# A scan kernel over 16 groups: the state's product one turn later, the skip term as the output bank's seed, GpSimd's root late in the step, x times last factors on VectorE

## The chip, the cores and the metric

The kernel runs on one core of a Trainium2 chip. The metric is the device time of one execution in microseconds (us); lower is better. Five things work side by side: TensorE (PE; PEld is its weight load), VectorE (DVE), ScalarE (ACT), GpSimd (POOL), and the DMA queues, all issued by SyncE (SP). Each engine takes its instructions in program order, and waits on semaphores where it needs another's result.

## What is computed

A layer norm, then a Mamba-2 mixer, gated by a LoRA feed-forward branch, for 2 sequences of 1024 tokens with 512 channels (64 heads of 64, 8 groups, state 128):

```python
xn = _layernorm(x)
proj = einsum('bld,pd->blp', xn, in_proj_w)            # gate, x | B | C, dt
xBC = silu(causal_conv4(x | B | C) + conv_bias)
dt = softplus(dt + dt_bias); dA = exp(dt * -exp(A_log))
state = state * dA_t + (dt_t * x_t) outer B_t          # for every token t
y_t = state @ C_t
y = y + x * D                                          # the skip term
yn = rms_norm_over_group(y) * norm_weight * silu(gate)
out = x + (yn @ out_proj_w.T) * silu(ffn(xn))
```

## The kernel before

The recurrence is worked out in chunks of 128 tokens. A batch's 8 groups times 8 chunks, for 2 batches, are N = 128 turns; turn i is chunk `i % NCH` (NCH = 8) of group `i // NCH`. One loop over i is written out once for each engine, and only the order in it and the semaphores' counts decide what runs when. Inside turn i the engines also work on m = i - 1 (mixing, gating, state) and u = i - 2 (output projection, norm's scale).

For each turn:

- GpSimd computes `skip` (x times D), splits new weights into a high and a low part on some turns (`split_out` at `i % 8 == 1`, `split_conv_x` at 3, `split_gate` at 4 and 6, `split_conv_bc` at 5), computes `xw` (`scale_x`: x times each head's last decay factor), `cpre` (`left_of_state`: C times decay from the chunk's start), adds up the squares of y in two additions (`sum1`, `sum2`), takes the root (`rstd_col`, a power of -0.5) and decays the state (`sdec`).
- TensorE runs the output projection of u (`ps_out`, twelve products), the mixing product of m into the bank `ps_y` (decay matrix times `dtx`, plus `cpre` times the state before), the product of B and C (G, half of `ps_g`), the sum of squares (another part of `ps_g`), one or two blocks of the input projection for the convolution (`ps_conv`, "early" and "late", on `i % 4 != 0` and `i % 4 != 3`), a gate block (`ps_gate`) and the state's product (`ps_s`: `xw` with B, not where `i % 8 == 7`).
- ScalarE evicts a late convolution block of the turn before (L692, L693), writes the mean square (L813), Silu, eight step sizes times x (`dtx`, L831), Square of y (L841), evicts the early block, copies y's high part (`ynt_hi`), the gate's Silu; on `i % 8 == 0` it scales the new output weights (L861), on 1 splits their high part (L645), and so for the other weights.
- VectorE does the taps of the convolution (L914, three), the scan that makes the decay matrix (L1049), the last factors (`last`, L1056), a transpose (L922), y plus skip (L1091), the new state (L1097), y times gate (L1104), the scaled output added to `out_sum` (L1130, waits for `ps_out` and `rstd_col`), y's low part (`ynt_lo`, semaphore `lo2`, L1136), the early taps, and M: the decay matrix times G (L1069), which is what the next mixing product reads.

"Step k" is in this text the stretch that begins when TensorE starts the mixing product in turn i, with i mod 8 = k, and ends when it starts the next one.

`xw`, `skip`, `ps_y` and `ps_s` are single buffers. The product of the state is written for turn i:

```python
w.wait_ge(S["xw"], inner(i))
w.wait_ge(S["state"], inner(m) if m >= 0 else 0)
e.matmul(ps_s[:, :], b_tok[i % 2][:, :], xw[:, :], start=True, stop=True).then_inc(S["mm_u"], 1)
```

SyncE's queue brings decay rows (`fetch_decays`), the rows for `cpre` (`fetch_rows`), and takes x to token order through memory (`store_turned`, `fetch_tokens`: `x_tok`, `b_tok`).

## Time and profile before

| | |
|---|---|
| runs | 1863.41 us median of 3 (1862.56 to 1866.68) |
| profiled execution | 1867.85 us, span of its instructions 1866.0 us |
| TensorE busy | 1733.9 us (93%), mean granted clock 0.981 |
| VectorE busy | 1480.7 us (79%) |
| GpSimd busy | 1307.5 us (70%) |
| ScalarE busy | 1021.8 us (55%) |
| DMA | 163 GB/s mean |

An engine's share is of the whole span. TensorE's granted clock is 1.0 at 2.4 GHz. "idle before <-releaser" gives how long an engine stood ahead of an instruction and what ended it; "issue" means that the profile shows nothing.

### The profile page before, as it was taken

The page shows a single profiled execution, that of the slowest core. Times are in us where ns is not written, and L with a number is a line of the kernel's source. Part 1 is how long each engine was busy: PE and PEld are TensorE (multiplying, and loading weights), DVE is VectorE, ACT ScalarE, POOL GpSimd, SP SyncE. Part 2 cuts the span into 40 slices and gives each one's busy share as a digit, 9 for nine tenths or more (in the row PEclk, how much of TensorE's full clock was granted, in tenths as well). Part 3 has the DMA queues.
Part 4 walks back from the last instruction along what each step waited for, and adds up shares of the span by engine and source line. Part 5 has one row for each costly group of instructions (what it writes and reads, how often), then busy time and mean ns, then how long its engine had stood idle before and what let it go on. Part 6 is the DMA issues. An engine that isn't in the chain of part 4 may idle for free.

```text
span 1866.0 us, 31464 instructions
## 1 busy us (share of the span) xinstructions
PE 1733.9 (93%) x10792; PEld 1375.5 (74%) x10792; DVE 1480.7 (79%) x1839; ACT 1021.8 (55%) x2715; POOL 1307.5 (70%) x1255
## 2 busy tenths in 40 slices
PE   8979989999998999999888998999999899999986
PEld 5757767777777877777777787777777777777865
DVE  7858788787878878787877887878788787878886
ACT  4555555655555565555645655465555546555544
POOL 6537668686767858676797857669585766958576
PEclk9989999999999999999999999999999999999989
DMA  8445545555454555455775654546355454635445
GB/s 265 145 143 167 168 142 172 143 165 149 147 169 147 170 151 160 144 155 167 221 243 177 180 163 150 164 146 189 110 177 156 145 163 146 187 112 166 150 139 184
DMA packets 322415, 304.76 MB, mean 163 GB/s; under 512 B 88272, under 2 KB 255568, under 8 KB 322256
## 3 DMA queue, kind: packets, MB, share of 16 engines
q1 hardware_dynamic: 321216, 302.60, 54.1%
q8 instruction: 86, 1.41, 0.3%
q14 instruction: 73, 0.60, 0.1%
q10 hardware_dynamic: 1040, 0.16, 0.0%
HBM read 246.57 MB, written 56.10 MB: 162 GB/s over the span
## 4 chain that ended last, share of the span: by engine, by line
PE 75%; DVE 9%; issue 8%; ACT 4%; POOL 2%; DMA 2%; SPq 1%; ACTq 0%; DVEq 0%; POOLq 0%
PE ps_conv L1345 9%; PE ps_conv L1348 8%; PE ps_y L1507 6%; PE ps_conv L1351 6%; PE ps_s L1537 6%; PE ps_gate L1345 5%; PE ps_out L1348 5%; PE ps_out L1345 5%; PE ps_gate L1348 5%; PE ps_y L1512 5%; PE ps_out L1351 4%; PE ps_gate L1351 4%; DVE xc L914 2%; PE ps_conv L1352 2%; ACT dtx L831 2%
## 5 line engine op out<-in xcount | busy, mean ns | idle before, releaser
L914 DVE SCALAR_TENSOR_TENSOR xc<-ps_conv,convw_sb,xc 128x511 f32<-128x511 f32 (+2 forms) x576 | 430.4, 747 | 221.5 <-ACT xc L693 207.9
L1276 POOL TENSOR_TENSOR rstd_col<-mean_square,half 128x1 f32<-128x1 f32 x128 | 111.6, 872 | 435.8 <-ACT mean_square L813 435.6
L1049 DVE TENSOR_TENSOR_SCAN decay<-decay,eye 128x1024 f32<-128x1024 f32 x125 | 293.6, 2349 | 0.0
L813 ACT ACTIVATE mean_square<-ps_g,eps 128x1 f32<-128x1 f32 x128 | 33.4, 261 | 453.0 <-PE ps_g L1338 453.0
L1255 POOL TENSOR_TENSOR cpre<-cpre,xc 128x1024 f32<-128x1024 f32 x112 | 267.9, 2392 | 0.0
L831 ACT ACTIVATE dtx<-x_tok,prefix_dt 128x64 f32<-128x64 f32 x1024 | 257.4, 336 | 8.6 <-DMA b_tok<-turned_d 8.6
L1345 PE MATMUL ps_conv<-xn_hi,wconv_hi 128*128 128x512 f32 x768 | 258.5, 460 | 0.0
L1348 PE MATMUL ps_conv<-xn_hi,wconv_lo 128*128 128x512 f32 x768 | 214.4, 402 | 0.0
L1537 PE MATMUL ps_s<-xw,b_tok 128*128 128x512 f32 x224 | 125.4, 643 | 95.4 <-issue 75.7
L1507 PE MATMUL ps_y<-decay,dtx 128*64 128x128 f32 x1984 | 191.5, 280 | 5.0 <-DVE decay L1069 5.0
L1345 PEld LDWEIGHTS ps_conv<-xn_hi,wconv_hi 128*128 128x128 f32 x768 | 143.5, 197 | 56.6 <-issue 31.3
L699 ACT ACTIVATE xc<-xc 128x512 f32<-128x512 f32 x192 | 120.0, 627 | 112.7 <-DVE xc L914 112.7
L1348 PEld LDWEIGHTS ps_conv<-xn_hi,wconv_lo 128*128 128x128 f32 x768 | 151.0, 197 | 34.9
L1512 PE MATMUL ps_y<-cpre,state 128*64 128x128 f32 x1760 | 171.5, 273 | 0.0
L1351 PE MATMUL ps_conv<-xn_lo,wconv_hi 128*128 128x512 f32 x576 | 163.5, 392 | 0.0
L1345 PE MATMUL ps_out<-wout_hi,ynt_hi 128*128 128x512 f32 x512 | 156.6, 427 | 6.4 <-issue 4.7
L1507 PEld LDWEIGHTS ps_y<-decay,dtx 128*64 128x64 f32 x1984 | 117.4, 137 | 50.4 <-issue 38.1
L1069 DVE TENSOR_TENSOR decay<-decay,ps_g 128x1024 f32<-128x1024 f32 x125 | 151.4, 1211 | 1.2 <-PE ps_g L1338 1.2
L693 ACT ACTIVATE xc<-ps_conv,convb_sb,convw_sb 128x512 f32<-128x512 f32 (+1 forms) x192 | 149.6, 779 | 0.0
L1348 PE MATMUL ps_out<-wout_hi,ynt_lo 128*128 128x512 f32 x512 | 138.5, 392 | 1.7 <-DVE ynt_lo L1136 1.7
L1345 PE MATMUL ps_gate<-xn_hi,wgate_hi 128*128 128x512 f32 x504 | 138.6, 397 | 0.0
L1299 POOL TENSOR_TENSOR square<-square 128x256 f32<-128x256 f32 x128 | 128.1, 1001 | 13.8 <-ACT square L841 13.8
(233 smaller groups left out, 3911.9 us busy)
## 6 DMA issues: line engine op xcount, KB each, us to landing
decay<-decays_d SPq DMA_DIRECT2D x125, 512.0 KB, 5.1
cpre<-rows_d SPq DMA_DIRECT2D x112, 512.0 KB, 3.8
turned_d<-squares SPq DMA_DIRECT2D x512, 80.0 KB, 2.0
stage<-w_in_t SPq DMA_DIRECT2D x32, 1024.0 KB, 5.2
x_tok<-turned_d SPq DMA_DIRECT2D x128, 256.0 KB, 3.2
stage<-w_out_t SPq DMA_DIRECT2D x16, 1024.0 KB, 5.4
stage<-w_in_t SPq DMA_DIRECT2D x32, 256.0 KB, 3.2
b_tok<-turned_d SPq DMA_DIRECT2D x128, 64.0 KB, 3.8
```

Of the source, the lines that this page charges most:

```text
L693: e.activation(acc[:, first:], ps[:, first:], ACT.Identity, bias=convb_sb[:, tile, 0:1], scale=tap).then_inc(S["tap0"], 1)
L831: scaled = e.activation(dtx[i % 2][:, h * HD:(h + 1) * HD].rearrange("p (a i) -> p a i", i=SQ), head_of(x_tok[i % 2], h), ACT.Copy, scale= ...
L914: e.scalar_tensor_tensor(acc[:, d:], ps[:, 0:BLK - d], convw_sb[:, tile, TAPS - 1 - d:TAPS - d], acc[:, d:], ALU.mult, ALU.add).then_inc(S ...
L1049: e.tensor_tensor_scan(d, d, eye8[:, :, :].rearrange("p h i -> p (h i)"), 0.0, ALU.mult, ALU.add).then_inc(scanned(i)[0], 1)
L1069: e.tensor_tensor(by_head(d), by_head(d), ps_g[:, P:2 * P].unsqueeze(1).to_broadcast([P, GH, P]), ALU.mult).then_inc(S["M"], 1)
L1255: e.tensor_tensor(cpre[k % 2][:, :, :], cpre[k % 2][:, :, :], xc[i // CPB % 2][:, XT + 1, block_cols(i % NCH)].unsqueeze(1).to_broadcast([ ...
L1345: e.matmul(ps, a_hi(t), b_hi_(t), start=t == 0, stop=False)
L1348: e.matmul(ps, a_lo(t), b_hi_(t), start=False, stop=False)
L1351: e.matmul(ps, a_hi(t), b_lo_(t), start=False, stop=False)
L1507: mixed = e.matmul(y_h, dx[:, h * HD:(h + 1) * HD], mx[:, h * P:(h + 1) * P], start=True, stop=cm == 0, skip_group_check=True)
L1512: mixed = e.matmul(y_h, before[:, h * HD:(h + 1) * HD], c_left[:, h, :], start=False, stop=True, skip_group_check=True)
L1537: e.matmul(ps_s[:, :], b_tok[i % 2][:, :], xw[:, :], start=True, stop=True).then_inc(S["mm_u"], 1)
```

## The change

Four edits. The state's product is issued in the turn after, for m instead of i, directly behind the mixing product. The skip term is no longer added by VectorE: ScalarE's new `seed(i)` copies `skip` into the output bank `y_bank(i)`, and the mixing product adds to it (`start=False`); Square and the state's update wait for the products alone. GpSimd's root stands behind the second addition of squares instead of at the turn's start, and `skip` at the turn's start instead of near its end. `scale_x` moves from GpSimd to VectorE, behind y times gate.

```diff
--- before.py
+++ after.py
@@ -799,6 +799,13 @@
                     for q, n in rate_part(s):
                         rate(q, part_of(q, n))
 
+            def seed(i):
+
+                w.wait_ge(S["skip"], i + 1)
+                w.wait_ge(S["lo2"], i if i <= TAIL else i - 1)
+                w.wait_ge(S["sgate"], CPB if i < TAIL else N)
+                e.activation(y_bank(i)[:, :], skip[:, :], ACT.Copy).then_inc(S["seed"], 1)
+
             steps = prefix_dt[:, :, :].rearrange("p c i -> p (c i)")
             for i in range(N + DRAIN):
                 m, u = i - 1, i - DRAIN
@@ -832,7 +839,7 @@
                                               head_of(x_tok[i % 2], h), ACT.Copy, scale=steps[:, first + h:first + h + 1])
                     scaled.then_inc(S["dtx"], 1)
                 if 0 <= m < N:
-                    w.wait_ge(S["y"], m + 1)
+                    w.wait_ge(S["mm_in"], m + 1)
                     w.wait_ge(S["sum2"], m)
                     if m == 0:
                         w.wait_ge(S["mm_pt"], 2)
@@ -1069,6 +1077,16 @@
                 e.tensor_tensor(by_head(d), by_head(d), ps_g[:, P:2 * P].unsqueeze(1).to_broadcast([P, GH, P]),
                                 ALU.mult).then_inc(S["M"], 1)
 
+            def scale_x(i):
+
+                w.wait_ge(landed_tok[i % 2], 32 * (i // 2 + 1))
+                w.wait_ge(*lasts(i))
+                w.wait_ge(S["biased"], TOK)
+                w.wait_ge(S["mm_u"], inner(i) - 1)
+                weight = last_room(i)[:, :, :].rearrange("p (t h) a -> p t (h a)", t=XT)
+                e.tensor_tensor(xw[:, :].rearrange("p (t a i) -> p t a i", t=XT, a=QUADS), x_of(x_tok[i % 2]),
+                                weight.unsqueeze(3).to_broadcast([P, XT, QUADS, SQ]), ALU.mult).then_inc(S["xw"], 1)
+
             for i in range(N + DRAIN):
                 m, u = i - 1, i - DRAIN
                 cm = m % NCH
@@ -1085,10 +1103,6 @@
                         scan(i)
                     if i + 1 < N:
                         turn(i + 1)
-                if 0 <= m < N:
-                    w.wait_ge(S["mm_in"], m + 1)
-                    w.wait_ge(S["skip"], m + 1)
-                    e.tensor_tensor(y_bank(m)[:, :], y_bank(m)[:, :], skip[:, :], ALU.add).then_inc(S["y"], 1)
                 if 0 <= m < N and cm < NCH - 1:
                     new = state[(group(m) + cm) % 2]
                     w.wait_ge(S["mm_u"], inner(m))
@@ -1102,6 +1116,8 @@
                     w.wait_ge(S["square"], m + 1)
                     w.wait_ge(S["sgate"], m // CPB * CPB + CPB)
                     e.tensor_tensor(turns(y_bank(m)), turns(y_bank(m)), gate_of(m), ALU.mult).then_inc(S["yg"], 1)
+                if i < N and i % NCH < NCH - 1:
+                    scale_x(i)
                 if TAIL < i < N:
                     mixing_matrix(i)
                 if u >= 0:
@@ -1256,24 +1272,18 @@
                                 xc[i // CPB % 2][:, XT + 1, block_cols(i % NCH)].unsqueeze(1).to_broadcast(
                                     [P, GH, P]), ALU.mult).then_inc(S["cpre"], 1)
 
-            def scale_x(i):
...
             for i in range(N + DRAIN):
                 m, u = i - 1, i - DRAIN
                 f = finished(i)
-                if u >= 0:
-                    col = slice(u % 2, u % 2 + 1)
-                    w.wait_ge(S["var2"], u + 1)
-                    w.wait_ge(S["osum"], u - 1)
-                    e.tensor_tensor(rstd_col[:, col], mean_square[:, col], half[:, :], ALU.pow).then_inc(S["rstd2"], 1)
+                if i < N:
+                    nb, gi = i // CPB, group(i) % GROUPS
+                    w.wait_ge(S["silu"], max(conv_no(nb, t) for t in range(XT)) + 1)
+                    w.wait_ge(S["par"], 128)
+                    w.wait_ge(S["seed"], i)
+                    w.wait_ge(S["biased"], TOK)
+                    e.tensor_tensor(turns(skip), xc[nb % 2][:, 0:XT, block_cols(i % NCH)],
+                                    dskip_sb[:, gi * XT:(gi + 1) * XT].unsqueeze(2).to_broadcast([P, XT, P]),
+                                    ALU.mult).then_inc(S["skip"], 1)
                 if i < N:
                     g, at = divmod(i, NCH)
                     left = BATCH * GROUPS - 1 - g
@@ -1300,6 +1308,12 @@
                     w.wait_ge(S["sum1"], m + 1)
                     w.wait_ge(S["mm_ssq"], m)
                     e.tensor_tensor(square_sum[:, :], square[:, 0:P], square[:, P:2 * P], ALU.add).then_inc(S["sum2"], 1)
+                if u >= 0:
+                    col = slice(u % 2, u % 2 + 1)
+                    w.wait_ge(S["var2"], u + 1)
+                    w.wait_ge(S["osum"], u - 1)
+                    e.tensor_tensor(rstd_col[:, col], mean_square[:, col], half[:, :], ALU.pow).then_inc(S["rstd2"], 1)
+                if 0 <= m < N:
                     if cm < NCH - 2:
                         new, dec = state[(group(m) + cm) % 2], state[(group(m) + cm + 1) % 2]
                         w.wait_ge(S["state"], inner(m))
@@ -1313,15 +1327,6 @@
                         first = (cm + 1) * HEADS + gm * GH
                         e.tensor_tensor(by_head(dec[:, :]), by_head(new[:, :]), heads_bc(total_bc[:, first:first + GH]),
                                         ALU.mult).then_inc(S["sdec"], 1)
-                if i < N:
-                    nb, gi = i // CPB, group(i) % GROUPS
-                    w.wait_ge(S["silu"], max(conv_no(nb, t) for t in range(XT)) + 1)
-                    w.wait_ge(S["par"], 128)
-                    w.wait_ge(S["y"], i)
-                    w.wait_ge(S["biased"], TOK)
-                    e.tensor_tensor(turns(skip), xc[nb % 2][:, 0:XT, block_cols(i % NCH)],
-                                    dskip_sb[:, gi * XT:(gi + 1) * XT].unsqueeze(2).to_broadcast([P, XT, P]),
-                                    ALU.mult).then_inc(S["skip"], 1)
                 if i < N and i % NCH == 0:
                     edges(group(i))
                 if f is not None and not on_vector(f):
@@ -1492,11 +1497,8 @@
                 if 0 <= m < N:
                     mx, dx = decay_room(m), dtx[m % 2]
                     w.wait_ge(S["M"], m + 1)
-                    w.wait_ge(S["sgate"], CPB - 1)
                     w.wait_ge(S["dtx"], m + 1)
-                    w.wait_ge(S["lo2"], m if m < TAIL else m - 1)
-                    if m >= TAIL:
-                        w.wait_ge(S["sgate"], N)
+                    w.wait_ge(S["seed"], m + 1)
                     if cm > 0:
                         w.wait_ge(S["state"], inner(m - 1))
                         w.wait_ge(S["cpre"], later(m))
@@ -1504,7 +1506,7 @@
                     for two in range(0, GH, 2):
                         for h in (two, two + 1):
                             y_h = y_bank(m)[h % 2 * HD:(h % 2 + 1) * HD, h // 2 * P:(h // 2 + 1) * P]
-                            mixed = e.matmul(y_h, dx[:, h * HD:(h + 1) * HD], mx[:, h * P:(h + 1) * P], start=True,
+                            mixed = e.matmul(y_h, dx[:, h * HD:(h + 1) * HD], mx[:, h * P:(h + 1) * P], start=False,
                                              stop=cm == 0, skip_group_check=True)
                         if cm > 0:
                             for h in (two, two + 1):
@@ -1512,6 +1514,12 @@
                                 mixed = e.matmul(y_h, before[:, h * HD:(h + 1) * HD], c_left[:, h, :], start=False,
                                                  stop=True, skip_group_check=True)
                     mixed.then_inc(S["mm_in"], 1)
+                if 0 <= m < N and cm < NCH - 1:
+                    w.wait_ge(S["pt"], len(RATES))
+                    w.wait_ge(landed_tok[m % 2], 32 * (m // 2 + 1))
+                    w.wait_ge(S["xw"], inner(m))
+                    w.wait_ge(S["state"], inner(m - 1) if m > 0 else 0)
+                    e.matmul(ps_s[:, :], b_tok[m % 2][:, :], xw[:, :], start=True, stop=True).then_inc(S["mm_u"], 1)
                 if i < N:
                     w.wait_ge(S["silu"], max(conv_no(i // CPB, t) for t in (XT, XT + 1)) + 1)
                     w.wait_ge(S["var2"], u if u >= 0 else 0)
@@ -1526,16 +1534,7 @@
                     conv(conv_early(i))
                 for k in gated(i):
                     gate(k)
-                late_first = i < N and conv_early(i) is None and conv_late(i) is not None
-                if late_first:
-                    conv(conv_late(i))
-                if i < N and i % NCH < NCH - 1:
-                    w.wait_ge(S["pt"], len(RATES))
-                    w.wait_ge(landed_tok[i % 2], 32 * (i // 2 + 1))
-                    w.wait_ge(S["xw"], inner(i))
-                    w.wait_ge(S["state"], inner(m) if m >= 0 else 0)
-                    e.matmul(ps_s[:, :], b_tok[i % 2][:, :], xw[:, :], start=True, stop=True).then_inc(S["mm_u"], 1)
-                if i < N and conv_late(i) is not None and not late_first:
+                if i < N and conv_late(i) is not None:
                     conv(conv_late(i))
 
 
```

TensorE in the second group, at a turn with `i % 4 == 3`. Before, the state's product (`ps_s`) stands behind the gate block and ahead of the output projection:

```order
L1345 MATMUL ps_gate<-xn_hi,wgate_hi 128x512 [waits s_sgate]
L1345 MATMUL ps_gate<-xn_hi,wgate_hi 128x512 x3
L1348 MATMUL ps_gate<-xn_hi,wgate_lo 128x512 x4
L1351 MATMUL ps_gate<-xn_lo,wgate_hi 128x512 x3
L1352 MATMUL ps_gate<-xn_lo,wgate_hi 128x512
L1537 MATMUL ps_s<-xw,b_tok 128x512 [waits s_state,s_xw,s_landed_tok1]
L1345 MATMUL ps_out<-wout_hi,ynt_hi 128x512 [waits s_hi2,s_osum]
L1345 MATMUL ps_out<-wout_hi,ynt_hi 128x512 x3
L1348 MATMUL ps_out<-wout_hi,ynt_lo 128x512 [waits s_lo2]
```

After, between the mixing product of m (`ps_y`) and G (`ps_g<-xc`):

```order
L1509 MATMUL ps_y<-decay,dtx 64x128 x2
L1514 MATMUL ps_y<-cpre,state 64x128 x2
L1522 MATMUL ps_s<-xw,b_tok 128x512 [waits s_xw,s_landed_tok0]
L1342 MATMUL ps_g<-xc 64x128 [waits s_var2]
L1343 MATMUL ps_g<-xc 64x128
L1342 MATMUL ps_g<-ones,square_sum 64x1 [waits s_sum2]
L1343 MATMUL ps_g<-ones,square_sum 64x1
L1350 MATMUL ps_conv<-xn_hi,wconv_hi 128x512 [waits s_taps]
L1350 MATMUL ps_conv<-xn_hi,wconv_hi 128x512 x3
```

It has moved ahead of both products into `ps_g`, and no longer waits for the state's update there.

GpSimd in the turn with `i % 8 == 3` (`wconv_lo` is the split of the convolution's weights). Before, root first, then splits, `xw`, `cpre`, the additions, `state`, `skip`:

```order
L1276 TENSOR_TENSOR rstd_col<-mean_square,half 128x1 [waits s_osum,s_var2]
L1156 TENSOR_TENSOR wconv_lo<-stage,wconv_hi 128x512 [waits s_hi_cx] x4
L1266 TENSOR_TENSOR xw<-x_tok,last 128x512 [waits s_mm_u,s_last,s_landed_tok1]
L1255 TENSOR_TENSOR cpre<-cpre,xc 128x1024 [waits s_landed_rows0]
L1299 TENSOR_TENSOR square<-square 128x256 [waits s_square]
L1302 TENSOR_TENSOR square_sum<-square 128x128 [waits s_mm_ssq,s_sum1]
L1314 TENSOR_TENSOR state<-state,total_bc 128x512 [waits s_sdec,s_mm_in,s_state]
L1322 TENSOR_TENSOR skip<-xc,dskip_sb 128x512 [waits s_y]
```

After, the row of `skip` first:

```order
L1284 TENSOR_TENSOR skip<-xc,dskip_sb 128x512 [waits s_seed]
L1172 TENSOR_TENSOR wconv_lo<-stage,wconv_hi 128x512 [waits s_hi_cx] x4
L1271 TENSOR_TENSOR cpre<-cpre,xc 128x1024 [waits s_landed_rows0]
L1307 TENSOR_TENSOR square<-square 128x256 [waits s_square]
L1310 TENSOR_TENSOR square_sum<-square 128x128 [waits s_mm_ssq,s_sum1]
L1315 TENSOR_TENSOR rstd_col<-mean_square,half 128x1 [waits s_osum,s_var2]
L1328 TENSOR_TENSOR state<-state,total_bc 128x512 [waits s_sdec,s_mm_in,s_state]
L1284 TENSOR_TENSOR skip<-xc,dskip_sb 128x512 [waits s_seed,s_silu]
```

The root has moved behind the splits, `cpre` and both additions; `xw` is gone from this engine.

ScalarE at the turn with `i % 8 == 0` (`stage<-stage,normw_sb` scales the output weights). Before:

```order
L841 ACTIVATE square<-ps_y 128x512 [waits s_sum2,s_y]
L848 ACTIVATE ynt_hi<-ps_y 128x512 [waits s_mm_out,s_yg]
L757 ACTIVATE sgate<-ps_gate 128x512 [waits s_mm_gate]
L861 ACTIVATE stage<-stage,normw_sb 128x512 [waits s_landed_stage0]
L861 ACTIVATE stage<-stage,normw_sb 128x512 x3
L692 ACTIVATE xc<-ps_conv,edge,convw_sb 128x1 [waits s_skip,s_edge_sum,s_mm_in,s_mm_conv]
L692 ACTIVATE xc<-ps_conv,edge,convw_sb 128x1 x2
L693 ACTIVATE xc<-ps_conv,convb_sb,convw_sb 128x509
L813 ACTIVATE mean_square<-ps_g,eps 128x1 [waits s_rstd2,s_mm_ssq]
```

After:

```order
L848 ACTIVATE square<-ps_y 128x512 [waits s_sum2,s_mm_in]
L855 ACTIVATE ynt_hi<-ps_y 128x512 [waits s_mm_out,s_yg]
L757 ACTIVATE sgate<-ps_gate 128x512 [waits s_mm_gate]
L807 ACTIVATE ps_y<-skip 128x512 [waits s_lo2,s_skip]
L869 ACTIVATE stage<-stage,normw_sb 128x512 [waits s_landed_stage0]
L869 ACTIVATE stage<-stage,normw_sb 128x512 x3
L692 ACTIVATE xc<-ps_conv,edge,convw_sb 128x1 [waits s_edge_sum,s_mm_conv]
L692 ACTIVATE xc<-ps_conv,edge,convw_sb 128x1 x2
L693 ACTIVATE xc<-ps_conv,convb_sb,convw_sb 128x509
L820 ACTIVATE mean_square<-ps_g,eps 128x1 [waits s_rstd2,s_mm_ssq]
```

The copy into `ps_y`, which waits for `lo2`, stands ahead of the weights' scaling and of the late convolution block's eviction (`xc<-ps_conv`).

## Rows read from the trace of the kernel before

**Rows 1.** Waits: engine, tile, line <- releaser: total us, times, longest.
```profile
PE ps_s L1537 <- issue: 75.7, 43, 3.1
...
PE ps_s L1537 <- POOL xw L1266: 19.7, 5, 7.5
```

**Rows 2.** Timeline (start us, us, instruction): starts of the mixing product.
```profile
452.01 0.76 PE L1507 MATMUL ps_y<-decay,dtx 128*64 128x128 f32 x9
...
470.20 0.44 PE L1507 MATMUL ps_y<-decay,dtx 128*64 128x128 f32 x4
...
484.39 0.44 PE L1507 MATMUL ps_y<-decay,dtx 128*64 128x128 f32 x4
...
498.07 0.44 PE L1507 MATMUL ps_y<-decay,dtx 128*64 128x128 f32 x4
...
560.94 0.55 PE L1507 MATMUL ps_y<-decay,dtx 128*64 128x128 f32 x6
```

**Rows 3.** Timeline of step 1 on TensorE; stretch of it: PE busy, granted clock.
```profile
456.16 1.07 PE L1345 MATMUL ps_gate<-xn_hi,wgate_hi 128*128 128x512 f32 x4
...
462.12 1.10 PE L1537 MATMUL ps_s<-xw,b_tok 128*128 128x512 f32 x2 [3.08 <-issue]
...
462.66 1.99 PE L1345 MATMUL ps_conv<-xn_hi,wconv_hi 128*128 128x512 f32 x4
...
462.70:466.20 3.50, 3.50 (x11) 0.60 0.57 153
```

**Rows 4.** Timeline of step 7, four engines.
```profile
538.50 0.44 PE L1507 MATMUL ps_y<-decay,dtx 128*64 128x128 f32 x4
...
539.00 2.28 DVE L1049 TENSOR_TENSOR_SCAN decay<-decay,eye 128x1024 f32<-128x1024 f32 x1
...
540.80 0.26 ACT L813 ACTIVATE mean_square<-ps_g,eps 128x1 f32<-128x1 f32 x1 [4.06 <-PE ps_g L1338]
...
541.13 0.55 POOL L1276 TENSOR_TENSOR rstd_col<-mean_square,half 128x1 f32<-128x1 f32 x1 [4.52 <-ACT mean_square L813]
...
543.39 0.58 ACT L841 ACTIVATE square<-ps_y 128x512 f32<-128x512 f32 x1
...
544.00 0.70 DVE L1104 TENSOR_TENSOR ps_y<-ps_y,sgate 128x512 f32<-128x512 f32 x1 [0.37 <-ACT square L841]
...
544.61 0.74 DVE L1130 SCALAR_TENSOR_TENSOR out_sum<-ps_out,rstd_col,out_sum 128x512 f32<-128x512 f32 x1
...
544.87 0.47 POOL L1302 TENSOR_TENSOR square_sum<-square 128x128 f32<-128x128 f32 x1
...
545.98 2.31 DVE L914 SCALAR_TENSOR_TENSOR xc<-ps_conv,convw_sb,xc 128x511 f32<-128x511 f32 x3
...
548.20 1.21 DVE L1069 TENSOR_TENSOR decay<-decay,ps_g 128x1024 f32<-128x1024 f32 x1
...
549.47 0.44 PE L1507 MATMUL ps_y<-decay,dtx 128*64 128x128 f32 x4 [0.34 <-DVE decay L1069]
```

**Rows 5.** Timeline: the state's product and what follows it, step 6.
```profile
532.07 1.02 PE L1537 MATMUL ps_s<-xw,b_tok 128*128 128x512 f32 x2
532.52 1.49 PE L1345 MATMUL ps_conv<-xn_hi,wconv_hi 128*128 128x512 f32 x4
```

**Rows 6.** Timeline: GpSimd in step 1; ScalarE in step 0.
```profile
453.77 2.29 POOL L1276 TENSOR_TENSOR rstd_col<-mean_square,half 128x1 f32<-128x1 f32 x1 [4.30 <-ACT mean_square L813]
...
456.03 4.99 POOL L1156 TENSOR_TENSOR wout_lo<-stage,wout_hi 128x512 fp32r<-128x512 f32 x4
...
556.15 2.55 ACT L861 ACTIVATE stage<-stage,normw_sb 128x512 f32<-128x512 f32 x4
...
559.31 0.78 ACT L693 ACTIVATE xc<-ps_conv,convb_sb,convw_sb 128x509 f32<-128x509 f32 x1
```

**Rows 7.** Timeline: GpSimd and VectorE at the end of step 3.
```profile
494.12 2.41 POOL L1255 TENSOR_TENSOR cpre<-cpre,xc 128x1024 f32<-128x1024 f32 x1
...
495.90 2.79 DVE L1049 TENSOR_TENSOR_SCAN decay<-decay,eye 128x1024 f32<-128x1024 f32 x1
```

12 lines of the change are left out of this document (2 added, 10 removed).

## Prediction

> **What bounds the kernel now.** I read the shares of busy time first, then the chain of waits, then one group of eight steps in the timeline. The shares (table above) put TensorE at 93%, so what can be won lies in the 132 us in which it is idle. The waits say where those are: 75.7 + 19.7 = 95.4 us in front of the state's product `ps_s` [rows 1]. The timeline shows the pattern, and it repeats from group to group: a group lasts 560.94 - 452.01 = 108.93 us, and 16 of them make up the kernel [rows 2]. In step 1 TensorE stands 3.08 us before `ps_s`, because GpSimd first does the root, then four splits (4.99 us), then `xw` [rows 3, 6]. It also pays afterwards: between 462.70 and 466.20 the granted clock is 0.60, so partly at the lower of 1.2 and 2.4 GHz, and the first four products of the block take 1.99 us where four take 1.07 us at full clock. The next four fall into the same stretch: at a mean clock of 0.6 its 3.5 us hold 2.1 us of work, and with `ps_s` and the block's end I put the loss at 1.9 us. Step 1 therefore loses some 5.1 us. Step 3 lasts 498.07 - 484.39 = 13.68 us [rows 2]; its like without a wait, step 7 with the state's product in it, would last 10.97 - 0.34 + 0.87 = 11.5 us, so it loses 2.2 us at the same product. Steps 1 and 3 make 3.08 + 2.2 = 5.3 us of idleness a group, 85 of the 95.4 us, so the others lose next to nothing.
>
> The second limit is less visible. In step 7, where there is no `ps_s` and no wait for it, the mixing product at 549.47 starts right behind VectorE's `decay` times `ps_g` (call it M), which ended at 549.41. So a short step is already set by a loop: mixing product, mean square, step sizes times x, Square, gate's product, sum into `out_sum`, taps, M, next mixing product. It takes 10.97 us [rows 4].
>
> **The change, part by part.**
>
> *The state's product behind the mixing product.* It now uses `xw` of the turn before, long ready. The wait in steps 1 and 3 goes: 5.1 + 2.2, and the few tenths of step 5 and of the 0.34 ahead of step 0's mixing product, at most 8.0 us a group. But the product now stands ahead of G and of the sum of squares. Its price is from its start to the next product's, 0.45 us, plus what that next group of four is longer, 1.49 - 1.07 = 0.42: 0.87 us [rows 5]. The mean square on ScalarE, and all of the loop behind it, starts 0.87 us later in steps 1 to 7.
>
> *The skip as seed.* VectorE loses 128 additions, about as long as the gate's product of the same shape, 0.70 us, ScalarE gains 128 copies; I price them by Square, which moves as much between the same memories, 0.58 us [rows 4]. The addition lay in the shadow of ScalarE's step sizes (Square ended at 543.97 and the gate's product followed at once), so nothing is won there. ScalarE's copy waits for `lo2`. In most steps this hides under its wait for the taps; in step 0 it does not, see below. Accumulating instead of starting costs TensorE nothing: the same products with another flag.
>
> *x times last factors on VectorE.* 112 products leave GpSimd and join VectorE between the gate's product and the sum into `out_sum`. No row has it; the gate's product (0.70 us) is nearest and I take 0.7 us, bounds 0.58 (Square, ScalarE) and 1.25 (a quarter of the four splits, GpSimd) [rows 4, 6]. It is covered where the sum waits for the root, which is the case below.
>
> *The root late.* This is what I think decides. The sum into `out_sum` waits for the root. Before, the root was computed at 541.13, a step's start, and the sum followed the gate's product. Now the root stands behind both additions of squares, which wait for Square. From Square's end at 543.97 it is 0.90 to the start of the second addition (the first lies in between), that takes 0.47, the root 0.55: 1.9 us [rows 4].
>
> *Step 7, worked out.* Square ended 5.47 us after the mixing product and will end at 5.47 + 0.87 = 6.34. The root is there at 8.2. The sum started at 6.11 and will start at 8.2, 2.1 later. `lo2`, taps and M follow it without a gap, as they did; a few hundredths are lost to `ynt_hi` before. M ends at 12.9 instead of 10.9, and the step lasts 13.0 instead of 10.97: **+2.0**. The taps and M (2.31 and 1.21) are all still there.
>
> *Step 0.* There is no `ps_s` in it now and its loop has no taps: it becomes 11.47 (560.94 - 549.47) less 0.87, 10.6: **-0.9**. But in it ScalarE must now wait for `lo2` (at 8.2) with its copy before it scales the four parts of the output weights (2.55) and evicts the late convolution. Before, that eviction ended at 560.09, 0.85 before step 1 began [rows 6]. Now: 8.2 + 0.6 + 2.5 + 1.5 = 12.8, which is 2.2 us after step 1 began.
>
> *Step 1.* VectorE's taps thus run from 2.2 to 4.5, then Silu to 5.2. Then ScalarE splits the output weights, the first tile within 0.6, and GpSimd follows tile by tile, the first one blocked by VectorE's scan until 6.8, see next part: 7.9 for the first, 11.6 for the fourth (4.99 for four [rows 6]). `cpre` 2.4 [rows 7]: 14.0. Then the additions and the root: 15.7, or 16.4 if VectorE's new product gets in between. The output's product needs the sum of one turn earlier. TensorE came to the end of its gate block 7.0 us into step 1 (462.12 - 3.08 - 452.01) [rows 2, 3]; with `ps_s` ahead (0.87) and a block of twelve, three times 0.9 us, it reaches the output at 10.6, and stands some 5.4 us. From 16.0: sum 0.7, `lo2` 0.7, taps 2.2, M 1.2, and the mixing product at 20.8. Before it was 470.20 - 452.01 = 18.19: **+2.6**. If the eviction were not late, the same chain gives 17.7; with the clock low once more, up to 22. TensorE's slow block mostly runs beside the taps and M.
>
> *Step 3 and the port.* Where VectorE and GpSimd meet, one waits. The scan at 495.90 took 2.79 instead of 2.28 us, because `cpre` ran until 496.53 [rows 4, 7]; and GpSimd's root in step 1, which fell into the scan, took 2.29 us where it takes 0.55 in step 7 [rows 4, 6]. So each can hold the other up for a whole instruction, and whichever came second waited. The Trainium skill (SBUF — State Buffer, "SBUF: two separate sides") has it as an exclusive lock between a GpSimd instruction and a VectorE instruction with two inputs in SBUF. The trace agrees for the scan (2.79 against 2.28). By that rule the new product on VectorE, which has both inputs in SBUF, waits for GpSimd too, up to one split in step 1, 1.25 us: 16 times that is 20 us on top of the sum below, and no row here shows it.
>
> In step 3 the splits now follow the skip (1.04), which waits for the seed of step 2 (about 10.4): 11.5 + 5.0, that is 2.3 into step 3, then `cpre` to 4.7. The scan wanted to start at 3.0. The scan (2.28), last factors, transpose and state bring VectorE to the gate's product at 8.4 instead of 6.4, the sum comes at 9.8 instead of 8.2, M at 14.6, up to 15.4 with more blocking: 15.0 for 13.68, **+1.3**. The same meeting in steps 4 and 5, smaller: **+0.5** and **+0.7**. Steps 2 and 6 are 14.2 us of TensorE's own work and longer than the loop: 0.
>
> *Sum.* 2.6 + 1.3 + 0.5 + 0.7 + 2.0 - 0.9 = 6.2 us a group, 16 groups: 99 us. The profiled execution took 1867.85 us (span 1866.0) and would take 1967; it is 4.4 above the median of the runs. Predicted against the median 1863.41: **1960 us**, slower by 5%.
>
> **Rivals.**
>
> *The waits do not meet (slower, but little).* Scan and GpSimd do not fall on each other as I place them. Then step 1 is 1.7 longer, step 3 is 13.0 (-0.7), steps 4 and 5 give 0 and -0.4, 7 and 0 stay at 2.0 and -0.9: +1.7 a group, 27 us, 1890 us. For it: before, only two or three steps of a group show a blocked instruction. Against: GpSimd's splits now stand directly ahead of `cpre` and later in time. Chance 0.2, taken as 1880 to 1930.
>
> *Faster.* The one mechanism: the root comes early enough. TensorE needs it only at the output's product, about 8.7 us into a short step (10.97 + 0.87 less a block of 2.7, less the 0.34 of waiting) and 10.6 into step 1. If GpSimd had it by then everywhere, the 8.0 us a group would be won nearly whole: 1863 - 16 x 8.0 = 1735; half of it gives 1800. It speaks for it that GpSimd is rid of 112 instructions. Against it: in step 7 the root at 8.2 is inside the limit and the loop through M still gains 2 us; in step 1 it would have to move from 15.7 to 10.6, and 5 us of splits and 2.4 of `cpre` stand ahead of it. It decides from there. Chance 0.08.
>
> *No change.* The wait at `ps_s` is paid at the output's product for the same price, the other terms cancel: 1860 to 1867. Chance 0.03.
>
> *More than forecast.* The clock stays low after 5 us of idleness, with its blocks on the path, and the new product on VectorE waits for GpSimd in each step: 2 us more a group, over 1990. Chance 0.09.
>
> **How the numbers follow.** Forecast (1930 to 1990): 0.60; the rivals 0.2, 0.08, 0.03, 0.09. Leaving out the faster and the same ones and the upper end leaves 0.8 between 1880 and 2000. A change of 0.2% (3.7 us) is about what a measurement of this kernel can tell from none. Faster 0.08, same 0.03, slower 0.89.
>
> **What would show it.** In the changed kernel's profile: no wait left before `ps_s`; TensorE idle before the output's product in step 1, 5 us or more, released by VectorE's sum into `out_sum`, which waits for `rstd_col`; mean square 3.2 us after the mixing product instead of 2.3; the sum 8.2 after it in step 7; M ending directly ahead of the mixing product in steps 1, 3 and 7; scans over 2.3 us. I am wrong if the sum comes within 7 us in the short steps, or if step 1 is under 17 us.

## The result, and the profile after

The changed kernel takes 2025.26 us (median of 4 runs, 2022.62 to 2026.77) where the kernel before takes 1864.01 beside it: a ratio of 1.0862 with a 95% interval of 1.0843 to 1.0881, 161 us slower. The forecast had 1960, with 2000 as its upper end. The direction was right, the size too small by 65 us.

The page: busy time of each engine, share of the span, instructions.

```profile
PE 1813.2 (90%) x10792; PEld 1386.9 (69%) x10792; DVE 1608.5 (80%) x1823; ACT 1087.3 (54%) x2843; POOL 1176.2 (58%) x1143
```

GpSimd is busy 131 us less, VectorE 128 us more. TensorE has the same 10792 products and is busy 79 us longer; its mean clock fell from 0.981 to 0.957. The chain that ended last went 75% through TensorE before; now it goes 2% through TensorE and 38% through GpSimd.

Waits (total, times, longest), to be held against [rows 1]:

```profile
PE ps_out L1350 <- DVE out_sum L1146: 127.7, 47, 6.6
...
PEld ps_s L1522 <- issue: 19.8, 112, 0.3
PE ps_y L1509 <- DVE decay L1077: 24.8, 37, 1.2
```

TensorE's wait before the state's product is gone (75.7 + 19.7 us); 127.7 us at the output's product stand in its place.

The timeline, step 1 of one group (mixing product at 591.14, the next at 613.47), to be held against [rows 3, 6]:

```profile
592.17 1.13 PE L1522 MATMUL ps_s<-xw,b_tok 128*128 128x512 f32 x2
...
608.05 2.08 PE L1350 MATMUL ps_out<-wout_hi,ynt_hi 128*128 128x512 f32 x4 [5.94 <-DVE out_sum L1146]
...
613.47 0.44 PE L1509 MATMUL ps_y<-decay,dtx 128*64 128x128 f32 x4
...
601.44 1.80 DVE L1087 TENSOR_TENSOR xw<-x_tok,last 128x512 f32<-128x512 f32 x1
607.24 0.75 DVE L1146 SCALAR_TENSOR_TENSOR out_sum<-ps_out,rstd_col,out_sum 128x512 f32<-128x512 f32 x1 [4.00 <-issue]
...
610.73 1.21 DVE L1077 TENSOR_TENSOR decay<-decay,ps_g 128x1024 f32<-128x1024 f32 x1
...
596.92 5.77 POOL L1172 TENSOR_TENSOR wout_lo<-stage,wout_hi 128x512 fp32r<-128x512 f32 x4 [6.36 <-ACT wout_hi L645]
602.65 2.79 POOL L1271 TENSOR_TENSOR cpre<-cpre,xc 128x1024 f32<-128x1024 f32 x1
...
606.60 0.55 POOL L1315 TENSOR_TENSOR rstd_col<-mean_square,half 128x1 f32<-128x1 f32 x1
```

Read from the bottom: splits, `cpre` and the additions come first, the root starts 15.46 us into the step and ends at 16.01. The sum follows at 16.10, and TensorE, idle for 5.94 us, starts the output's product. The row of the sum names no releaser here ("issue"); that it is the root is read from the 0.09 us between them, and e1 below confirms it. M ends at 611.94, 20.80 into the step. But the mixing product starts at 22.33, when the output's twelve products are done. Stretches of TensorE in this step (us, busy PE, PEld, DVE, ACT, POOL, granted clock, DMA share, GB/s), the output's block first and one ahead of the wait second:

```profile
608.05:613.47 5.42, 5.42 (x13) 3.80 (x13) 4.38 (x6) 2.62 (x6) 3.49 (x3) 0.50 0.11 38
597.00:601.70 4.70, 4.70 (x22) 3.90 (x21) 4.14 (x6) 4.70 (x16) 4.70 (x4) 1.00 0.16 40
```

The block runs wholly at the lower of the two levels, 1.2 GHz, and takes 5.42 us; twelve such products took 2.72 us at 596.51 to 599.23.

The timeline of step 3 (627.98 to 643.60), to be held against [rows 7]:

```profile
639.34 1.20 PE L1350 MATMUL ps_out<-wout_hi,ynt_hi 128*128 128x512 f32 x4 [2.25 <-DVE out_sum L1146]
...
641.76 1.48 PE L1356 MATMUL ps_out<-wout_lo,ynt_hi 128*128 128x512 f32 x3
...
643.60 0.69 PE L1509 MATMUL ps_y<-decay,dtx 128*64 128x128 f32 x4
...
630.75 4.31 DVE L1057 TENSOR_TENSOR_SCAN decay<-decay,eye 128x1024 f32<-128x1024 f32 x1
...
637.49 1.14 DVE L1087 TENSOR_TENSOR xw<-x_tok,last 128x512 f32<-128x512 f32 x1
638.55 0.74 DVE L1146 SCALAR_TENSOR_TENSOR out_sum<-ps_out,rstd_col,out_sum 128x512 f32<-128x512 f32 x1
```

The scan takes 4.31 us, 2.03 more than in step 7: it starts beside GpSimd's `cpre` (630.54 to 632.92) and ends 2.1 us after it, as long as a scan takes alone. The sum waits here for VectorE's own queue, the new product in it. TensorE waits 2.25 us, and its block then runs its first four products at full clock and slows down from the second part on; the granted clock from 639.34 to 643.60 is 0.66.

The timeline of step 7 (685.32 to 698.71), to be held against [rows 4]:

```profile
688.28 0.32 PE L1342 MATMUL ps_g<-xc 128*64 128x128 f32 x1
...
694.76 1.20 PE L1350 MATMUL ps_out<-wout_hi,ynt_hi 128*128 128x512 f32 x4 [0.32 <-DVE out_sum L1146]
...
698.71 0.44 PE L1509 MATMUL ps_y<-decay,dtx 128*64 128x128 f32 x4 [0.93 <-DVE decay L1077]
...
688.83 0.26 ACT L820 ACTIVATE mean_square<-ps_g,eps 128x1 f32<-128x1 f32 x1 [4.00 <-PE ps_g L1343]
...
693.96 0.75 DVE L1146 SCALAR_TENSOR_TENSOR out_sum<-ps_out,rstd_col,out_sum 128x512 f32<-128x512 f32 x1 [1.23 <-POOL rstd_col L1315]
```

The mean square comes 3.51 us into the step (2.30 before), the sum 8.64 (6.11 before), and it waits for the root.

Step lengths in us, the median over the first 15 groups, of the main kernels:

| | 1 | 2 | 3 | 4 | 5 | 6 | 7 | 0 |
|---|---|---|---|---|---|---|---|---|
| before | 18.26 | 14.19 | 13.68 | 11.60 | 14.62 | 14.19 | 10.96 | 11.47 |
| changed | 22.10 | 14.53 | 15.87 | 12.29 | 14.77 | 14.49 | 13.39 | 11.00 |
| e1 | 15.47 | 14.49 | 14.97 | 12.31 | 14.49 | 14.49 | 12.17 | 10.57 |
| e3 | 18.85 | 15.75 | 16.16 | 11.51 | 14.19 | 14.19 | 13.19 | 11.47 |
| e2 | 13.88 | 14.51 | 13.41 | 11.77 | 14.49 | 14.49 | 12.17 | 10.57 |
| e4 | 22.25 | 14.16 | 14.59 | 12.26 | 14.88 | 14.15 | 12.17 | 10.98 |
| e5 | 13.72 | 14.15 | 13.75 | 12.59 | 14.15 | 14.15 | 11.56 | 10.58 |
| e6 | 20.94 | 14.51 | 15.44 | 12.34 | 14.78 | 14.49 | 13.40 | 10.99 |
| e9 | 14.97 | 15.66 | 16.03 | 11.43 | 14.15 | 14.62 | 12.22 | 10.56 |
| e14 | 13.73 | 15.63 | 14.53 | 11.42 | 14.15 | 14.15 | 11.56 | 10.56 |
| e15 | 21.86 | 14.65 | 14.70 | 11.86 | 14.49 | 14.49 | 13.38 | 10.65 |

The changed kernel's step lengths add up to 9.5 us a group more than before, 151 us in 16 groups. The two profiled executions differ by 157 us; the 6 between lie mostly in single steps away from the medians. The other 4 of the 161 are the 4 us by which the profiled execution of the kernel before was longer than the median of its runs.

### The profile page after: what moved, and what is told of

It is laid out like the page before. It is cut to its first block, busy times and chain, and to the rows that moved or that the text cites. A ratio compares the mean times of both kernels' runs of the same rounds, so it can differ in the third digit from the quotient of the medians.

```text
span 2022.8 us, 31468 instructions
## 1 busy us (share of the span) xinstructions
PE 1813.2 (90%) x10792; PEld 1386.9 (69%) x10792; DVE 1608.5 (80%) x1823; ACT 1087.3 (54%) x2843; POOL 1176.2 (58%) x1143
## 4 chain that ended last, share of the span: by engine, by line
POOL 38%; issue 33%; DVE 16%; ACT 9%; PE 2%; DMA 1%; POOLq 0%; SPq 0%; ACTq 0%; DVEq 0%
POOL cpre L1271 12%; POOL skip L1284 5%; POOL wconv_lo L1172 5%; POOL square L1307 4%; POOL wout_lo L1172 4%; DVE ynt_lo L1152 4%; POOL wgate_lo L1178 4%; ACT ps_y L807 3%; DVE out_sum L1146 3%; DVE xc L922 3%; DVE xw L1087 2%; ACT stage L869 2%; POOL rstd_col L1315 1%; DVE ps_y L1118 1%; POOL square_sum L1310 1%
## 5 line engine op out<-in xcount | busy, mean ns | idle before, releaser
L1057 DVE TENSOR_TENSOR_SCAN decay<-decay,eye 128x1024 f32<-128x1024 f32 x125 | 362.7, 2902 | 0.0
L1307 POOL TENSOR_TENSOR square<-square 128x256 f32<-128x256 f32 x128 | 97.8, 764 | 426.9 <-ACT square L848 426.9
L1271 POOL TENSOR_TENSOR cpre<-cpre,xc 128x1024 f32<-128x1024 f32 x112 | 307.8, 2749 | 0.0
L1350 PE MATMUL ps_out<-wout_hi,ynt_hi 128*128 128x512 f32 x512 | 165.6, 450 | 151.5 <-DVE out_sum L1146 127.7
L1284 POOL TENSOR_TENSOR skip<-xc,dskip_sb 128x512 f32<-128x512 f32 x128 | 133.4, 1042 | 196.0 <-ACT ps_y L807 190.2
L1350 PEld LDWEIGHTS ps_out<-wout_hi,ynt_hi 128*128 128x128 f32 x512 | 99.0, 208 | 201.8 <-DVE out_sum L1146 159.3
L1350 PE MATMUL ps_conv<-xn_hi,wconv_hi 128*128 128x512 f32 x768 | 217.7, 405 | 0.0
L807 ACT ACTIVATE ps_y<-skip 128x512 f32<-128x512 f32 x126 | 75.8, 602 | 231.0 <-DVE ynt_lo L1152 231.0
L1146 DVE SCALAR_TENSOR_TENSOR out_sum<-ps_out,rstd_col,out_sum 128x512 f32<-128x512 f32 x108 | 80.8, 748 | 130.8 <-issue 113.9
L1353 PE MATMUL ps_out<-wout_hi,ynt_lo 128*128 128x512 f32 x512 | 160.1, 441 | 1.9 <-DVE ynt_lo L1152 1.8
```

Of the source, the lines that this page charges most:

```text
L1057: e.tensor_tensor_scan(d, d, eye8[:, :, :].rearrange("p h i -> p (h i)"), 0.0, ALU.mult, ALU.add).then_inc(scanned(i)[0], 1)
L1271: e.tensor_tensor(cpre[k % 2][:, :, :], cpre[k % 2][:, :, :], xc[i // CPB % 2][:, XT + 1, block_cols(i % NCH)].unsqueeze(1).to_broadcast([ ...
L1284: e.tensor_tensor(turns(skip), xc[nb % 2][:, 0:XT, block_cols(i % NCH)], dskip_sb[:, gi * XT:(gi + 1) * XT].unsqueeze(2).to_broadcast([P, ...
L1307: e.tensor_tensor(square[:, 0:2 * P], square[:, 0:2 * P], square[:, 2 * P:], ALU.add).then_inc(S["sum1"], 1)
L1350: e.matmul(ps, a_hi(t), b_hi_(t), start=t == 0, stop=False)
L1353: e.matmul(ps, a_lo(t), b_hi_(t), start=False, stop=False)
```

## The experiments

Two theories stood at the start. The first: the root behind the additions keeps the sum, and with it TensorE, waiting. The rival: the root's place is cheap, and the cost lies in the state's product ahead of G, in the new product on VectorE, and in the clock. Each kernel is compared with the kernel before on the same chip (medians 1864 to 1867 us); intervals are 95%. A difference between two of the other kernels is that of their medians, which for some pairs come from two chips.

**The root's place.** In e1 the changed kernel has it first in GpSimd's turn again, ahead of `skip`; in e3 the kernel before has nothing but this edit.

```diff
+                if u >= 0:
...
+                    e.tensor_tensor(rstd_col[:, col], mean_square[:, col], half[:, :], ALU.pow).then_inc(S["rstd2"], 1)
                 if i < N:
                     nb, gi = i // CPB, group(i) % GROUPS
```

> The changed kernel with one part undone: GpSimd's root stands first in its turn again, ahead of skip. Theory R (the root behind the splits, cpre and the additions costs most, together with the low clock that TensorE's long wait brings): step 1 falls from 22.1 to about 17.5 us, because the sum into out_sum starts behind the new product on VectorE at 12.1 instead of 16.05; steps 3 and 7 fall by 2 to 3 and by 1.2; in all some 7 to 10 us a group, 1865 us, between 1840 and 1920. Theory L (the state's product in front of G and of the squares, 1.2 us later in every loop, and the port shared with the new product on VectorE cost most): the root's place gives at most 1 us a group, 2005 us or more.

> The kernel before with one part alone: GpSimd's root behind the two additions of squares. Theory R: in step 1 the root moves from 4 to about 14 us into the step, but TensorE is late there anyway for xw, so that it costs some 1 to 2 us, steps 3 and 7 0.5 to 1.1 each: 3 to 4 us a group, 1910 to 1930 us. It is also seen in VectorE waiting for rstd_col ahead of out_sum. Theory L: the root's place costs nothing, 1860 to 1875 us.

Measured: e1 1881.34 us, ratio 1.0072 (1.0055 to 1.0088), clock 0.988; e3 1985.80 us, 1.0635 (1.0620 to 1.0651). The late root costs 119 us by itself and 144 within the change: the first theory holds. e3 cost more than I expected, and not in step 1, where it loses 0.6 us and 1 to 2 were expected. Steps 2, 3 and 7 lose 1.6, 2.5 and 2.2 us; 0.5 to 1.1 were expected of 3 and 7 and nothing of 2. In e3's list of waits the sum waits for the root almost every time:

```profile
DVE out_sum L1130 <- POOL rstd_col L1302: 279.5, 108, 6.1
```

In step 1 TensorE is late for `xw` anyway, as in the kernel before, so that little of the late root shows. Its timeline there shows both:

```profile
595.69 1.10 PE L1538 MATMUL ps_s<-xw,b_tok 128*128 128x512 f32 x2 [3.01 <-POOL xw L1266]
596.22 2.15 PE L1346 MATMUL ps_conv<-xn_hi,wconv_hi 128*128 128x512 f32 x4
...
599.09 0.55 POOL L1302 TENSOR_TENSOR rstd_col<-mean_square,half 128x1 f32<-128x1 f32 x1
```

**The state's product.** e2: that edit alone on the kernel before. e5: the same, but behind the sum of squares. e4: the changed kernel with it there.

```diff
                 if 0 <= u < N - 1:
                     sum_squares(u)
+                if 0 <= m < N and cm < NCH - 1:
...
+                    e.matmul(ps_s[:, :], b_tok[m % 2][:, :], xw[:, :], start=True, stop=True).then_inc(S["mm_u"], 1)
                 if TAIL < i:
```

> The kernel before with one part alone: the state's product in the turn after, directly behind the mixing product. Theory R: the waits of 3.1 and 2.2 us and the low clock after the first go, the loop is 1.2 us longer where it binds (step 7, part of step 3): -4.3, -0.9, +1.2, -0.8 us, 5 us a group less, about 1785 us (1760 to 1820), faster than before. Theory L: the 1.2 us come back in each of the eight steps and eat the gain: 1860 us or more.

> The kernel before with the state's product in the turn after, behind G and the sum of squares. Theory R with the loop: against the product in front of G (1815 us) the mean square starts 1.2 us sooner, steps 1, 3 and 7 shrink by 0.7 to 1.2 us, and steps that TensorE fills by 0.3 (14.49 to 14.16): about 4 us a group, 1755 us (1740 to 1775). If the loop is not what binds steps 1, 3 and 7 there, only the 0.3 us: 1795 us or more.

> The changed kernel with the state's product two positions later, behind G and the sum of squares, so that the mean square starts at 2.3 instead of 3.5 us into a step; all else as changed. Theory L: 1.2 us less in each of at least six steps, 7 us a group, 1910 us. Theory R: it helps only where the loop from the mean square binds, 1.2 us in steps 1, 7 and partly 3, 3 us a group, 1975 us (1950 to 2000).

Measured: e2 1815.30 us, 0.9721 (0.9707 to 0.9736); e5 **1805.79 us**, 0.9674 (0.9658 to 0.9690), the fastest of the study; e4 1981.67 us, 1.0611 (1.0595 to 1.0627). So this edit is a gain, 52 us alone, and its place ahead of G costs: 10 us in e2 against e5, 44 us in the changed kernel, where steps 3 and 7 fall by 1.3 and 1.2 us without it and steps 2 and 6 by 0.3 to 0.4. G starts 1.79 us into a step of e5 (559.25 to 561.04) and 2.96 into step 7 of the changed kernel: 1.17 us, not the 0.87 of the forecast. I had expected 1755 for e5. Against e2, step 1 gains only 0.2 us where 0.7 to 1.2 were expected, and steps 3 and 4 lose 0.3 and 0.8. Its timeline in step 3 (573.40 to 587.15):

```profile
576.03 2.61 POOL L1276 TENSOR_TENSOR rstd_col<-mean_square,half 128x1 f32<-128x1 f32 x1 [4.36 <-ACT mean_square L813]
578.62 5.05 POOL L1156 TENSOR_TENSOR wconv_lo<-stage,wconv_hi 128x512 fp32r<-128x512 f32 x4
583.62 1.06 POOL L1266 TENSOR_TENSOR xw<-x_tok,last 128x512 f32<-128x512 f32 x1
584.63 2.38 POOL L1255 TENSOR_TENSOR cpre<-cpre,xc 128x1024 f32<-128x1024 f32 x1
...
587.15 0.44 PE L1507 MATMUL ps_y<-decay,dtx 128*64 128x128 f32 x4 [1.66 <-POOL cpre L1255]
```

GpSimd has no gap from the root to `cpre`, and the mixing product waits 1.66 us for `cpre`: with the one wait gone, GpSimd's queue is what binds in step 3. The root in it takes 2.61 us for 0.55, beside VectorE's scan, which ends at 578.30.

**The clock.** e6 puts 26 (turn 2 of 8) or 10 (turn 4) useless products into a bank that is free then, ahead of the output's product, so that TensorE does not stand idle. The outputs do not depend on them.

```diff
                 if 0 <= u and i <= TAIL:
+                    for _ in range({2: 26, 4: 10}.get(i % NCH, 0) if group(i) != 7 and i > NCH else 0):
+                        e.matmul(turned_x[:, :], wgate_hi[:, 0, 3 * P:], xn_hi[:, 0, 0:BLK], start=True, stop=True)
                     output(u)
```

> The changed kernel with products that compute nothing needed (the high gate weights on themselves, into a bank that is free) ahead of the output's product, 26 on turns with i mod 8 = 2 and 10 with i mod 8 = 4, so that TensorE works while it waits for the sum into out_sum. Every wait of the other engines stays. Theory C (the clock that falls after the long wait is the missing part): the output blocks in steps 1 and 3 take 2.8 instead of 4.8 and 4.5 us at a granted clock of 1.00, step 1 falls to about 20.8 us, where VectorE's M ends, step 3 to 15.3, 1.9 us a group, 1995 us. If the clock is not it: no change or slower, 2025 us or more.

Measured: 2009.22 us, 1.0768 (1.0748 to 1.0788), clock 0.987. Its timeline in step 1 (588.22 to 609.14), and behind it the stretch's row:

```profile
599.70 5.38 PE L1497 MATMUL turned_x<-xn_hi,wgate_hi 128*128 128x512 f32 x23
605.19 1.21 PE L1350 MATMUL ps_out<-wout_hi,ynt_hi 128*128 128x512 f32 x4
...
609.14 0.44 PE L1511 MATMUL ps_y<-decay,dtx 128*64 128x128 f32 x4 [0.89 <-DVE decay L1077]
```

```profile
604.20:609.14 4.94, 3.93 (x17) 2.55 (x15) 4.63 (x6) 1.75 (x5) 3.74 (x4) 1.00 0.24 61
```

The clock stays at 1.00, and the mixing product waits for M again, as forecast: step 1 takes 20.94 where 20.8 was said. So the slow block was on the path. It cost 1.16 us in step 1 and 0.43 in step 3 by the medians, and 16 us in all; I had expected 30.

**The seed.** e7: the seed alone, `skip` first in GpSimd's turn with it (the change's own lines for `seed`, `skip` and `start=False`). e12: e2 with the seed, which is e1 without the factors on VectorE, but for `skip` standing ahead of the root.

> The kernel before with one part alone: the skip as seed of the output's bank, and skip itself first in GpSimd's turn (it has to be there for the seed). All theories: the addition on VectorE lay beside ScalarE's work, so nothing is won in steps 2 to 7; in step 0 the copy waits for lo2 ahead of the weights' scaling and the late eviction, the high part of the output weights comes about 1.3 us later in step 1 and xw with it: +1.3 us a group, 1885 us (1865 to 1900). If the addition did bind: under 1860 us.

> The kernel before with the state's product directly behind the mixing product (alone 1815 us) and the skip as seed. The late eviction in step 0 moves the taps of step 1 by 1.5 us, and no wait for xw hides that now: step 1 from 13.9 to 15.4, 24 us, 1840 us (1830 to 1855). If the seed costs what it cost alone: 1825 us. What is left to the 1881 us of the kernel with the root first is the new product on VectorE.

Measured: e7 1877.16 us, 1.0062 (1.0046 to 1.0079); e12 1823.03 us, 0.9775 (0.9753 to 0.9798). The seed costs some 10 and 8 us, most of it in step 1 (18.69 for 18.26; 14.53 for 13.88). The forecast had nothing for it but the late eviction out of step 0, at 3.1 us of step 1 (20.8 instead of 17.7). With the root early it costs 0.4 and 0.65 us there. No run takes the seed out of the changed kernel, so its price beside the late root is not known.

**The factors on VectorE.** e8: that edit alone (`scale_x` behind y times gate). e9: e5 with it. e10: e9 with the seed. e13: the changed kernel with `scale_x` on GpSimd, at the end of its turn. In the diff (e8) VectorE's lines come first, then GpSimd's, where it stood ahead of `cpre`.

```diff
+                if i < N and i % NCH < NCH - 1:
+                    scale_x(i)
...
-                if i < N and i % NCH < NCH - 1:
-                    scale_x(i)
```

> The kernel before with one part alone: x times last factors on VectorE, behind y times gate; root and state's product where they were. xw then no longer stands behind the splits on GpSimd: the wait before the state's product falls from 3.1 and 2.2 to 0 to 2 us, with it the low clock in step 1; step 1 15 instead of 18.2 us, step 3 12.5 instead of 13.7, about 1795 us (1780 to 1830). Theory P (the port that VectorE and GpSimd share makes the product wait for a split each time and the loop longer): 1.2 us and more in steps 1, 3 and 7 come back, 1830 us or more.

> The kernel before with two parts: the state's product behind the sum of squares (alone 1806 us) and x times last factors on VectorE behind y times gate (alone 1836 us). If the two add up: 1806 - 32 = 1774 us. Theory P (both took away the same wait, and the new product on VectorE costs the loop its 0.7 us or, where cpre runs, up to 2.5 us): no gain over the first alone, 1795 to 1820 us.

> The run before plus the skip as seed (alone +10 us): the whole change with the root first and the state's product behind the sum of squares. If the seed adds what it added alone: 10 us over the run without it. If its copy on ScalarE, which waits for lo2, meets a lo2 that the new product on VectorE has made later: 25 us or more over it. The changed kernel with the root first alone took 1881 us; with the product behind the squares it should fall by 25 to 45 us of that.

> The changed kernel with x times last factors on GpSimd again, but behind the state's decay, late in its turn, where no one waits for it. The root stays late. Theory R: the sum waits for the root in most steps, so that the product on VectorE was hidden; only steps 3 and 5, where it ran 1.1 and 1.4 us against GpSimd, gain: 25 us, 2000 us (1985 to 2025). Theory P (the shared port is the larger part): under 1960 us.

Measured: e8 1835.78 us, 0.9839 (0.9813 to 0.9865); e9 1886.88 us, 1.0108 (1.0084 to 1.0132); e10 1870.08 us, 1.0018 (1.0006 to 1.0030); e13 1977.62 us, 1.0603 (1.0588 to 1.0619). Alone the edit gains 32 us, because `ps_s` gets its `xw` earlier (step 1 takes 15.22 for 18.26). I had expected 1795; 1836 is in the range named for the port. Behind e5, which has no such wait, it costs 81 us, behind e12 (which with it is e1) 58, and in the change 48. One forecast for e9 added the gains of e5 and e8 up; they are the same wait, removed twice. The other, no gain and at most 1820 us, was 67 us short as well. e13 came 7 us under its range. That the seed helps e9 by 17 us was not expected. It costs 1.2 us in step 1 again, and steps 2, 3, 6 and 7, in which VectorE no longer adds the skip term, fall by 0.3 to 0.7; whether the missing addition does it was not tried.

**Why the product on VectorE costs so much.** e14: e9 with the last factors written into a free PSUM bank instead of SBUF, so the product has only one operand in SBUF. e15: the same in the changed kernel. e20: e14 with the product behind the sum into `out_sum`. e21: e20 with the seed.

```diff
-        last = [sb(f"last{i}", [P, GH, 2]) for i in range(3)]
+        last = [turned_x[:, 2 * GH * k:2 * GH * (k + 1)].rearrange("p (h a) -> p h a", a=2) for k in range(3)]
```

> The run with the state's product behind the squares and x times last factors on VectorE (1887 us), where the new product took 1.6 us in the median and up to 2.9, 0.68 at the least. Here the last factors stand in a free PSUM bank, so that the product has one input in SBUF and one in PSUM; order and waits are the same. Theory P (VectorE with two inputs in SBUF and GpSimd hold each other up): the product takes 0.7 us in all steps, steps 1, 2, 3 fall by about 1 us each, some 3 us a group, 1840 us (1825 to 1855). If its length comes from anything else (its access pattern, the token tiles): 1880 us or more.

> The changed kernel (2025 us), root late and all, with only the last factors in PSUM. Theory R: its product was mostly covered by the wait for the root; the gain is in step 3 (1.14 instead of 0.7) and 5: 5 to 15 us, 2010 to 2020. Theory P as the larger part: under 1980 us.

> The run with the factors in PSUM, and x times last factors one place later on VectorE, behind the sum into out_sum, where VectorE had stood 0.5 us for y's high part. If this gap covers most of the product: 0.5 us a step in steps 1, 3 and 7, 1.5 us a group, 20 to 30 us under the run with the product ahead of the sum, and at or under the 1806 us of the state's product alone. If not: the same as that run.

> As the run before, plus the skip as seed, that is all four parts of the change in a form in which the root is early, the product of the state is behind the squares and the port is avoided. The seed alone cost 10 us, with the state's product 8; here VectorE's addition (0.67 us) is in front of the taps in more steps, so that its loss may pay: between 10 us under and 10 us over the run without it.

Measured: e14 1825.59 us, 0.9785 (0.9767 to 0.9803); e15 1991.17 us, 1.0679 (1.0662 to 1.0696); e20 1823.82 us, 0.9777 (0.9762 to 0.9792); e21 1829.75 us, 0.9812 (0.9797 to 0.9826). One operand in PSUM gives back 61 us of e9's 81, and 34 in the changed kernel, where 5 to 15 were expected. e21 has all four parts of the change, with the root early, the state's product behind the squares and one operand in PSUM: it is 35 us faster than the kernel before, though still 24 slower than e5 alone. Groups of instructions (busy us, mean ns), first e9, then e14:

```profile
L1079 DVE TENSOR_TENSOR xw<-x_tok,last 128x512 f32<-128x512 f32 x112 | 173.3, 1548 | 3.2 <-DMA b_tok<-turned_d 3.2
```

```profile
L1079 DVE TENSOR_TENSOR xw<-x_tok,turned_x 128x512 f32<-128x512 f32 x112 | 75.9, 677 | 2.6 <-DMA b_tok<-turned_d 2.6
```

The same place in step 1 of each, in the timeline, first e9, then e14:

```profile
569.16 5.78 POOL L1168 TENSOR_TENSOR wout_lo<-stage,wout_hi 128x512 fp32r<-128x512 f32 x4 [1.61 <-ACT wout_hi L645]
...
573.84 1.65 DVE L1079 TENSOR_TENSOR xw<-x_tok,last 128x512 f32<-128x512 f32 x1
```

```profile
554.38 5.77 POOL L1168 TENSOR_TENSOR wout_lo<-stage,wout_hi 128x512 fp32r<-128x512 f32 x4 [1.39 <-ACT wout_hi L645]
...
559.06 0.68 DVE L1079 TENSOR_TENSOR xw<-x_tok,turned_x 128x512 f32<-128x512 f32 x1
```

Beside the same splits the product takes 1.65 us with both operands in SBUF and 0.68 with one in PSUM. Where nothing holds it up it takes 0.68 to 0.72 in e9 too, so PSUM itself does not make it faster.

In the changed kernel the product is held up in steps 1, 3 and 5. In steps 0, 2, 4 and 6 it is not, but there it holds GpSimd up, in the second addition, right ahead of the late root. Step 0 of the changed kernel, then of e15:

```profile
585.75 0.73 DVE L1087 TENSOR_TENSOR xw<-x_tok,last 128x512 f32<-128x512 f32 x1
586.00 0.80 POOL L1310 TENSOR_TENSOR square_sum<-square 128x128 f32<-128x128 f32 x1
```

```profile
580.32 0.68 DVE L1087 TENSOR_TENSOR xw<-x_tok,turned_x 128x512 f32<-128x512 f32 x1
580.58 0.47 POOL L1310 TENSOR_TENSOR square_sum<-square 128x128 f32<-128x128 f32 x1
```

The addition takes 0.80 us for 0.47, and root and sum come 0.33 us later (the sum 7.23 us into step 0, 6.90 in e15). The 20 us by which e14 still stands behind e5 are not the product's place in the loop: e20 moves it behind the sum and is no faster, where I had expected 20 to 30 us. They lie in steps 2 and 3 (15.63 and 14.53, for 14.15 and 13.75), less what step 4 gives (11.42 for 12.59). In step 2 of e14 the cause can be seen, and it is in `last`, whose inputs both still lie in SBUF:

```profile
567.57 2.28 DVE L1049 TENSOR_TENSOR_SCAN decay<-decay,eye 128x1024 f32<-128x1024 f32 x1
569.89 2.19 DVE L1056 TENSOR_TENSOR turned_x<-decay,prefix_dt 128x16 f32<-128x16 f32 x1
...
567.58 4.46 POOL L1267 TENSOR_TENSOR cpre<-cpre,xc 128x1024 f32<-128x1024 f32 x1
```

`cpre` starts with the scan and lasts that much longer; then `last`, 0.17 us elsewhere, takes 2.19 beside what is left of `cpre`. With `xw` gone from GpSimd, `cpre` comes earlier and meets them. That this is all of the 20 us was not tried.

## Why the prediction had the direction right and the size wrong

*What bounds the kernel: right. What the first edit gives back: right in step 1 only.* Before `ps_s` only 0.2 us is left each time (19.8 us in 112). The forecast had it give back at most 8.0 us a group. e5, with the root early, gives back 4.5 in step 1 (5.1 forecast), nothing in step 3 (2.2 forecast), where GpSimd's queue binds instead, and 62 us in all, 3.9 a group. So the rival "faster", 1735 us if GpSimd had the root in time everywhere, was priced wrong too: e2 and e5, with the root early, take 1815 and 1806. The forecast never said what each edit is worth alone; two of the four, e2 and e8, are gains alone.

*The root late: right, and the largest part.* The mechanism was forecast in order and in numbers: the root done 15.7 us into step 1 (16.01), the sum at 16.0 (16.10), an idle time of 5.4 (5.94; the forecast counted it to the sum's start, and TensorE waits for its end), M's end at 20.8 (20.80), the late eviction's taps at 2.2 (593.34 is 2.20). The last is partly luck: `lo2` came 0.4 us later than forecast in step 0, and the step was 0.4 us longer. e1 and e3 show the root as the cause, 144 and 119 us. One sign did not come: M ends directly ahead of the mixing product in step 7 alone; in steps 1 and 3 the output's block ends last.

*"TensorE's slow block mostly runs beside the taps and M": this step failed.* Step 1 is the step that misses most, by 1.2 of 3.3 us a group. It left the clock out of the sum, though the text had "up to 22" for it. The block of twelve takes 5.42 us at clock 0.50, from 608.05, so it ends 1.5 us after M. Step 1 came out at +3.8 instead of +2.6; e6 takes 1.16 of that away.

*The price of `ps_s` ahead of G: mis-sized.* 0.87 was taken from a place ahead of a convolution block [rows 5]. Between the mixing product and G it is 1.17. The 0.3 us more are in steps 2 and 6 too, which were put at 0: 14.53 and 14.49 for 14.19. Those steps were no cover for it: they are TensorE's own work, and the same product costs more there. In step 7 it turns +2.0 into +2.4.

*Step 3: mis-sized.* The sum was put at 9.8 and came at 10.57: the scan was held for 2.0 us instead of 1.7, `last` took 0.53 us for 0.17, and VectorE's new product took 1.14 instead of 0.7. M was put at 14.6 and ended at 15.26, and the mixing product came 0.36 us after it, behind the slow block (clock 0.66). +1.3 was +2.2. In e15, where the product takes 0.67 us, TensorE waits 1.63 us instead of 2.25, its block runs at full clock (1.00 from 632.55 to 635.60), and step 3 takes 14.70 for 15.87: the sum comes 0.6 us earlier and the step is 1.2 us shorter, the clock with it. e13, without the product on VectorE, has 14.22.

*The port: a term that should have stood in the sum.* The forecast took the product as 0.7 us, covered where the sum waits for the root, and left the rest to a rival. The product took 1.06 us in the mean (0.67 to 2.64 us), and it is not covered: held or not, it makes the sum later, in the even steps by holding GpSimd's addition ahead of the root. Its second operand in PSUM wins 34 us. The Trainium skill (SBUF — State Buffer, "SBUF: two separate sides") has a lock between a GpSimd instruction and a VectorE instruction with two inputs in SBUF; these runs agree with it for the new product too (1.65 against 0.68).

*Step 0* was put at -0.9 and came at -0.5; e13 and e15, without the product on VectorE or with its operand in PSUM, have 10.66 and 10.65 for 11.00, so most of the difference is that product, which holds the addition ahead of the root (0.80 us for 0.47). *Steps 4 and 5* were put at +0.5 and +0.7 and came at +0.7 and +0.15. In a group the steps 1, 2, 3, 6, 7 and 0 miss by 1.2, 0.3, 0.9, 0.3, 0.4 and 0.4 us, 4 and 5 by 0.2 and -0.55; unrounded that adds up to the 3.3 us between the 6.2 of the forecast and the 9.5 measured. What happened is nearest to the rival "more than forecast", put at 0.09 and at 2 us more a group: both of its parts are there, the clock (16 us, e6) and the product beside GpSimd (34 us, e15), though the product is held up in three steps only and not in each. These two overlap in step 3, where the product costs the clock too, and the price of `ps_s` was in no rival.

## What to carry to other kernels

Ask of a small instruction what its result releases, not what it takes: 0.55 us of root, put 5 to 10 us later in its turn, costs 119 us. A long wait takes TensorE's clock with it wherever it is moved, so its block behind the wait is priced at the lower level (5.42 us for 2.72 here, behind 5.94 us) and set against what runs beside it. A product on VectorE beside GpSimd is priced both ways: what holds it, and what it holds. Two gains that remove the same wait do not add up (e5 and e8), so an edit is priced in the company that it will have.

## What the runs showed of the hardware that was not expected

- A block of twelve products of 512 columns behind 5.94 us of idle time ran wholly at a granted clock of 0.50 and took 5.42 us for 2.72. Behind 2.25 us of idle time the first four ran at 1.00 and the rest slower, 0.66 in all; behind 1.63 us (e15) all ran at 1.00. Useless products in the gap kept it at 1.00 (e6).
- A VectorE product of 128x512 with both inputs in SBUF takes 0.68 to 2.94 us beside GpSimd's work (e9), and 0.68 us in the mean of 112 with one in PSUM (e14).
- The holding goes both ways: GpSimd's addition of 128x128 takes 0.80 us beside such a product and 0.47 with one operand in PSUM.
- GpSimd and VectorE hold each other up in turn: a scan and `cpre` that start together, then `last`, took 2.28, 4.46 and 2.19 us, where `cpre` and `last` take 2.38 and 0.17 alone.
- A product of 512 columns between two groups of 64-row products cost 1.17 us, and 0.87 ahead of a convolution block [rows 5].
